# Known-weight matmuls into banks that are overwritten later, at twelve places between the attention's last rounds and the third shared unit

## The reference, cut to what matters

```
x = layernorm(x + attention(x))                       # 16 heads of 16 channels, over 32 sequences of 128
x = layernorm(x + cross_attention(ctx, ctx, x))       # one head
h = rmsnorm(x) ; x = x + attention3(h) @ wo           # the third attention, 16 heads, no biases
h2 = rmsnorm(x)
combine = top 2 of 8 experts per token, softmax of the router's logits h2 @ router_w
moe = swiglu_shared(h2) + sum_e combine[:, e] * swiglu_e(h2)
x = layernorm(x + moe)
```

## Time and profile before

| what | value |
|---|---|
| median of 3 runs | 1093.47 us (1090.72, 1093.47, 1093.68) |
| the profiled execution, its own time | 1091.65 us |
| its span, first to last instruction | 1089.8 us |
| PE busy | 1010.1 us (93%) |
| PEld busy | 943.0 us (87%) |
| DVE busy | 845.9 us (78%) |
| ACT busy | 679.9 us (62%) |
| POOL busy | 519.9 us (48%) |
| mean granted TensorE clock | 0.971 of full speed |

### The profile page before, as it was taken

One profiled execution on the slowest core, in us unless ns is written; L12 is line 12 of the kernel. 1 busy time (PEld: TensorE's weight loads), 2 busy tenths in 40 slices (PEclk: granted clock), 3 DMA queues, 4 the chain that ended last, 5 costly groups with the idle time before them and its releaser, 6 DMA issues. The chain is left out here.

```text
span 1089.8 us, 30349 instructions
## 1 busy us (share of the span) xinstructions
PE 1010.1 (93%) x11710; PEld 943.0 (87%) x11710; DVE 845.9 (78%) x1564; ACT 679.9 (62%) x1435; POOL 519.9 (48%) x539
## 2 busy tenths in 40 slices
PE   5789999999999999999766899999999999999984
PEld 4678888888888888887555799999999999999984
DVE  2758888988888998898745886878888888885445
ACT  2346566766766676677644335778777777775335
POOL 4244554454565445455330143566676655663132
PEclk9999999999999999999976899999999999999988
DMA  7764445545454544433012306689888777771973
GB/s 208 141 119 79 82 77 101 112 95 107 100 108 82 106 109 98 97 72 108 31 50 74 89 20 222 220 252 335 288 263 263 244 252 259 259 238 56 215 171 116
DMA packets 273710, 161.22 MB, mean 148 GB/s; under 512 B 213472, under 2 KB 238944, under 8 KB 272928
## 3 DMA queue, kind: packets, MB, share of 16 engines
q1 hardware_dynamic: 262576, 127.62, 43.6%
q0 software_dynamic: 9408, 29.18, 10.1%
q10 hardware_dynamic: 1584, 2.49, 0.7%
HBM read 120.54 MB, written 38.70 MB: 146 GB/s over the span
## 5 line engine op out<-in xcount | busy, mean ns | idle before, releaser
L1896 POOL DMA_INDIRECT kept_weights<-h_scratch,source_row x71 | 99.1, 1396 | 112.4 <-DVE tok_lo L1743 84.4
L1905 POOL DMA_INDIRECT results_scratch<-kept_late,result_row x71 | 95.2, 1340 | 50.5 <-ACT kept_late L1459 34.6
L1441 ACT ACTIVATE act_hi<-prod 128x512 fp32r<-128x512 f32 x94 | 59.3, 631 | 75.5 <-DVE prod L1754 75.5
L1754 DVE TENSOR_TENSOR prod<-kept_weights,up 128x512 f32<-128x512 f32 (+1 forms) x112 | 71.6, 640 | 32.6 <-ACT kept_weights L1434 16.3
L693 ACT ACTIVATE p3t<-psum 128x512 f32<-128x512 f32 x128 | 67.7, 601 | 45.7 <-PE psum L539 45.7
L1412 ACT ACTIVATE we_hi<-w_raw 128x1024 fp32r<-128x1024 f32 x81 | 85.6, 1057 | 5.4 <-PE down L1343 5.4
L963 POOL TENSOR_TENSOR x_lo<-x_t,x_hi 128x512 fp32r<-128x512 f32 x16 | 20.5, 1279 | 142.4 <-ACT x_hi L599 142.3
L881 DVE TENSOR_REDUCE max<-psum 128x16 f32<-128x2048 f32 x32 | 73.3, 2290 | 5.1 <-PE psum L525 2.5
L1763 DVE TENSOR_TENSOR act_lo<-prod,act_hi 128x512 fp32r<-128x512 f32 x94 | 65.7, 699 | 13.7 <-ACT act_hi L1441 13.4
L384 PE MATMUL psum<-kept_room,x_hi 128*128 128x512 f32 (+1 forms) x256 | 63.3, 371 | 12.7 <-POOL x_lo L963 11.9
L1434 ACT ACTIVATE kept_weights<-gate 128x512 f32<-128x512 f32 (+1 forms) x112 | 62.3, 556 | 20.4 <-PE gate L1321 20.1
(11 more groups left out here) (335 smaller groups left out, 3476.9 us busy)
## 6 DMA issues: line engine op xcount, KB each, us to landing
w_raw<-in_w_gate SPq DMA_DIRECT2D x27, 512.0 KB, 4.0
w_raw<-in_w_up SPq DMA_DIRECT2D x27, 512.0 KB, 5.2
w_raw<-in_w_down SPq DMA_DIRECT2D x27, 512.0 KB, 6.4
raw_gate<-in_w_gate SPq DMA_DIRECT2D x13, 512.0 KB, 4.0
passed<-in_w_up SPq DMA_DIRECT2D x13, 512.0 KB, 5.4
passed<-in_w_down SPq DMA_DIRECT2D x13, 512.0 KB, 7.1
x_t<-in_x_t SPq DMA_DIRECT2D x16, 256.0 KB, 3.9
q_scratch<-qk SPq DMA_DIRECT2D x16, 256.0 KB, 2.3
```

Source lines behind the costliest of these rows:

```text
L1441: act.activation(act_hi[:, n % 2, h * FH:(h + 1) * FH, :], prod[:, h, :].rearrange("p (f n) -> p f n", f=FH), ACT.Copy).then_inc(act_hi_do ...
L1754: dve.tensor_tensor(used(prod[:, h, :], n), used(silu[:, h, :], n), used(up[h][:, :], n), ALU.mult).then_inc(prod_done, 1)
L1896: pool.indirect_dma_start(out=slot_rows[:, i % 2, j, :], out_offset=None, in_=by_token, in_offset=bass.IndirectOffsetOnAxis(ap=source_row[ ...
L1905: pool.indirect_dma_start(out=scratch["results"], out_offset=bass.IndirectOffsetOnAxis(ap=result_row[:, at:at + 1], axis=0), in_=y_rows[:, ...
```

## The change

Ahead of nine TensorE jobs of the last rounds, and of three halves of shared units, TensorE gets extra matmuls whose results nobody reads. In the first block each is a float32r product of 256 columns (`wo3`'s first 128 columns by `wo3`) into a bank, behind a wait that the bank's last user has been read; 7, 10, 22, 11, 32, 5, 5, 24 and 5 of them, 121 in all. In the second block each is a float32 product of 128 columns (the identity by itself) into `turned[0]`, without a wait; 24 calls ahead of `gate_up(0, 0)`, 8 ahead of `gate_up(1, 0)` and 28 ahead of `gate_up(2, 1)`. Nothing is removed and nothing is moved.

```diff
+LAST = PAIRS - 1
+FILLED = {("turn_h", LAST): (1, 7), ("s3_0", LAST): (0, 10), ("tm_0", LAST): (4, 22), ("s3t_1", LAST): (6, 11),
+          ("turn_h2", LAST - 1): (7, 32), ("logits", LAST - 1): (5, 5), ("out3", LAST): (6, 5), ("turn_h2", LAST): (7, 24),
+          ("logits", LAST): (5, 5)}
+FILLED_UNITS = {(0, 0): 24, (1, 0): 8, (2, 1): 28}
...
+                def fill(job, pair):
+
+                    b, times = FILLED[job, pair]
+                    order = in_order("pe")
+                    user, its_pair = [x for x in order[:order.index((job, pair))] if b in BANK[x[0]]][-1]
+                    after(pe, LAST_READ[user], its_pair)
+                    for _ in range(times):
+                        pe.matmul(psum[:, 512 * b:512 * b + D], w_hi["wo3"][:, 0, 0:P], w_hi["wo3"][:, 0, :], start=True, stop=True)
+
                 def step(job, pair):
                     prepare(job, pair)
+                    if (job, pair) in FILLED:
+                        fill(job, pair)
                     for other, its_pair in had_bank[job, pair]:
                         after(pe, LAST_READ[other], its_pair)
...
                 def gate_up(n, h):
                     k = 2 * n + h
                     w_hi, w_lo = weights_of(n)
+                    for _ in range(FILLED_UNITS.get((n, h), 0)):
+                        pe.matmul(turned[0][:, 0:P], ident[:, :], ident[:, :], start=True, stop=True)
                     if h == 0:
                         pe.wait_ge(tok_lo_done, n + 1)
```

## The result

| | before | after |
|---|---|---|
| median | 1092.10 us (1090.36 to 1093.68, 4 runs) | 1085.97 us (1084.88 to 1087.84, 4 runs) |
| profiled execution, span | 1091.65, 1089.8 us | 1084.88, 1083.0 us |
| PE busy, granted clock | 93%, 0.971 | 95%, 0.989 |

The ratio of the runs is 0.9963 with a 95% interval of 0.9946 to 0.9981: 0.4% faster, 4.0 us, or 2 to 6. The two medians, of four runs each, differ by 6.1 us, just beyond the upper end of that interval. The kernel became faster, by more than this measurement is uncertain, and the prediction of 1087.8 us in a range of 1084.8 to 1093.5 holds it.

What follows compares the result with a forecast made beforehand. TensorE bounds the kernel, partly at half clock after waits; VectorE sets the pace from 582 to 634 us. Gains of 5.90 less 0.25 give 5.65 us: median 1087.8, own range 1085 to 1090.5, with rivals 1084.8 to 1093.5.

Steps and rivals of the forecast that it cites:

- Fills of the first block, price and place: First block: each fill matmul takes 0.12 us at full clock; those with a row are shorter than their waits, costing nothing.
- Step 1: First block, last rounds: at full clock `s3t_0` starts at about 550.95 instead of 553.35 us, 2.40 us gained.
- step 2: First block, from `s3t_1` to `pv3_1`: 3.86 us at full clock instead of 5.39, 1.53 us gained.
- Step 3: First block, `pv3_1` to `out3` 15: evacuation, reciprocals and norms on other engines, so the 3.93 us gain carries over unchanged.
- Rival (C): Last rounds: another engine, there ScalarE, is the true pace; only 0 to 2.5 us come through, 1092 us; chance 0.12.
- All five steps: First block: gains of 2.40, 1.53, 1.16 (`out3` 15), 0.46 (`turn_h2` 15) and 0.35 (`logits`, `turn_lg` 15) sum to 5.90 us.
- a sign of being wrong: Whole kernel: the forecast would be wrong if the old median's executions lost more or less here than the profiled one.
- Second block, -0.25: Shared units: fills outlast their waits and `count_choices` ends 0.25 us late for VectorE's scan, costing 0.25 us in all.
- the upper bound's mechanism: Second block: the cost rises to 2 us if the fill starts at half clock.
- rival (A): Ahead of `out3` 15, behind `turn_lg` 14 or at block's end: clock falls once more, 0.1 us gain, 1093.4; chance 0.12.
- Third unit, no gain and no loss: Half (2, 1): fill and half end at 618.3 us, about as before, and VectorE wants it at 621.00; gains nothing.
- Sum: Whole kernel: 5.90 us gained in the first block less 0.25 in the second gives 5.65 us.

Runs made afterwards that it cites:

- e7: The changed kernel with only the fills ahead of `s3_0`, `tm_0` and `s3t_1` 15 (10, 22, 11), none ahead of the units; ratio to before 0.9980.
- e2: The changed kernel with only the fills ahead of the shared units, none in the first block; ratio to before 1.0014.
- e8: The changed kernel with one matmul in each of the nine first-block places, added waits kept, none ahead of the units; ratio to before 0.9991.
- e1: The changed kernel with the nine fills of the first block alone, none ahead of the shared units; ratio to before 0.9962.
- e3: The changed kernel with 12, 4 and 14 calls ahead of the units in place of 24, 8 and 28; ratio to before 0.9978.
- e4: The changed kernel with each first-block fill a float32 transpose of the identity, none ahead of the units; ratio to before 0.9961.
- e10: The changed kernel with first-block fills on all 128 rows and 32 columns, none ahead of the units; ratio to before 0.9944.
- e5: The changed kernel with each first-block fill twice as long, none ahead of the units; ratio to before 1.0045.
- e9: The changed kernel with first-block fills on 32 rows and all 128 columns, none ahead of the units; ratio to before 1.0014.

## Why the prediction was right, and where it was off

- **Fills of the first block, price and place:** 32 of them last 4.10 us (0.12 apart), 22 and 10 as planned; the waits around them shrank and none grew. Right, with one margin gone: the 24 of `turn_h2` 15 start 0.77 us late, behind the added semaphore wait, and leave no idle time ahead of their job.
- **Step 1,** `s3t_0` 2.40 earlier: from `s3_0` it was 553.35 - 542.37 = 10.98 and is 549.40 - 540.78 = 8.62, so 2.36. The copies of `neg_max` on VectorE are the new releaser, with 0.43 us of idle time, as foreseen.
- **Steps 1 and 2,** `pv3_1` 3.93 earlier: 562.09 - 542.37 = 19.72 and 556.60 - 540.78 = 15.82, so 3.90; e7, which has only these, gives 3.91 in the stretch. But 1.53 of it, step 2, stands on one execution. It is the price of the fall at 556.6, and that fall is absent in e2 and e8, where nothing fills the waits either: there `pv3_1` comes 18.05 and 17.98 behind `s3_0`, and fills earn 2.2 us up to it, all in step 1.
- **Step 3,** carried over: `out3` 15 from 28.84 to 25.00, 3.84. Rival (C), a gain hidden by ScalarE, is out.
- **All five steps,** 5.90: measured 39.88 - 33.97 = 5.91, and within 0.05 in e1, e3, e4 and e10. Both numbers come from the same profile of before. Against e2 and e8 (38.20 and 37.85) the gain is 4.2 and 3.9, and the whole runs agree with these: their ratios give 4.1 us (2.7 to 5.7) in e1, 4.2 (2.7 to 5.8) in e4, and in e7 the 2.2 of step 1 alone, where the steps gave 3.93. (e10's three runs, 6.1 with 2.9 to 9.3, can't tell.) So 5.90 is right for the profiled execution and, by these, 1.7 to 2 too large for most. How often the kernel before has the fall at 556.6 isn't shown, as it was profiled once. The prediction named this as a sign of being wrong, that the other executions of before lose less at this place; its profile had a mean clock of 0.971, and 53 of the 61 runs of before that were made beside the experiments had more.
- **Second block, -0.25:** measured -1.14 (52.25 to 53.39). This term was mis-sized too. The two records a call were right, and their spacing of 0.123 a little large (56 records from 601.98 to 608.14 are 0.110 each). But the fill ahead of unit 0 began at 1.00 and lost the clock at once, for 3.5 us: 7.0 us to the first gate matmul and not 5.9. VectorE's product came 0.93 late (10.23 for 9.30), its scan 1.11: the 0.25 forecast, 1.1 more for this fill, 0.26 less for the next (16 records in 1.70 and not 1.96). That was the upper bound's mechanism (2 us if the fill starts at half clock) at half its size, as in e2, where the fill did start at half clock and the middle stretch grew by 0.99, and the part of rival (A) that came true: the change of blocks had been named as an open place and priced into (A) alone.
- **Third unit, no gain and no loss:** right. With the clock at 0.59 there (e1) and at 1.00 (after, e3) the middle stretch is 52.2 to 52.4 where the fills are short or absent; VectorE is the pace.
- **Sum:** 5.65 forecast, 5.91 - 1.14 = 4.77 in the stretches. The profiled spans differ by 6.8, since after also had 1.59 less ahead of `s3_0` 15 and 0.4 behind the takeover, in work that is the same; the medians by 6.1. Medians of before beside the experiments were 1089.5 to 1091.3, so agreement of 1087.8 with 1085.97 to within 2 us is partly the chance of the runs. The ratio's interval, 2 to 6 us, is the sounder test. 5.65 and 4.77 lie in it, and so do the 3 us (4.2 or 3.9, less 1.14) that the usual execution of before would give: it can't tell them apart. The forecast was right in its mechanism, and in part lucky in its size.
- **Rival (A), a slip in its sum:** with 4.8 us of the fill at 0.43 a call and the rest at 0.245 it lasts 7.9 and not 8.1 us; this moves the rival by 0.2.

## What to carry to other kernels

Work that nobody reads pays where TensorE is itself late between waits and the waits have let its clock fall; here it gave about 4 us (5.9 against the one profiled execution of before), all of it in front of work that TensorE bounds. Where VectorE set the pace the fast clock was worth nothing. Where TensorE did, a fill longer than its wait cost nine tenths of the excess (e5), so fill a little less than the wait as the trace shows it, count the records that one call makes, and leave the units alone (e1). A fill could be a transpose or have 32 columns; with 32 rows it didn't help. And take more than one profile of the kernel before: what its waits cost differed by 2 us between executions, more than some steps of the sum.

## What the runs showed of the hardware

- With fills on 32 of 128 rows TensorE was busy without a gap and yet at 1.2 GHz (e9: 8.10 of 8.10 us at 0.50, the regular jobs between the fills unchanged); with fills on 128 rows and 32 columns it stayed at 2.4 GHz (e10: 1.00 from 541.7 to 566).
- With float32 transposes of an identity as fills it stayed there as with products (e4: 1.00 from 540 to 574).
- The same waits let the clock fall in one execution and not in another (before at 556.6, e2 and e8 not until past 562): the stretch without fills took 37.85, 38.20 and 39.88 us in three profiles (e8, e2, before), with fills that kept the clock 33.93 to 33.98 in five. Filling removed this spread too.
- A float32 product of 128 columns is two records, at full clock 0.106 to 0.110 us each in after (16 and 56 of them), so that a call takes nearly as long as two float32r products of 256 columns, 0.12 us each.
